# Ternary feed-forward block: the first layer of a group beside the second layer of the group before

## The reference, cut to what matters

```
W_fc: (1024, 256)   W_proj: (256, 1024)   ln_w, ln_b: (1024,)
absmean(W): gamma = mean(|W|) + 1e-6;  Ws = W / gamma
            sign(Ws) * min(round(|Ws|), 1)          # -1, 0 or 1
h = einsum('btd,hd->bth', layernorm(x), absmean(W_fc))
h = gelu(h, approximate=False)
h = (h - mean(h)) / sqrt(var(h) + 1e-5) * ln_w + ln_b
x = x + einsum('btd,dh->bth', h, absmean(W_proj))
```

## Time and profile before

| what | value |
|---|---|
| median of 3 runs | 3279.15 us (3278.52 to 3281.96) |
| profiled execution, its own time | 3280.81 us |
| span of its trace | 3278.7 us |
| mean granted TensorE clock | 0.904 of full speed |
| PE busy over the span | 2688.4 us (82%) |
| DVE, ACT, POOL busy | 1828.0, 1209.4, 793.0 us |
| block `l0f` in the trace | from 463.3 us to 680.4 us |

### The profile page before, as it was taken

How to read it: one execution, slowest core, us unless ns; L and a number is a source line. 1 busy time by engine, 2 the same in 40 slices (tenths; PEclk the granted TensorE clock), 3 DMA queues, 4 the chain that set the end, 5 groups by cost and what they waited for, 6 DMA issues and landing times. The chain is left out here.

```text
span 3278.7 us, 47320 instructions
## 1 busy us (share of the span) xinstructions
PE 2688.4 (82%) x15122; PEld 1841.3 (56%) x15123; DVE 1828.0 (56%) x3976; ACT 1209.4 (37%) x3052; POOL 793.0 (24%) x613
## 2 busy tenths in 40 slices
PE   3998977779777779599998979869867688879996
PEld 1565754457545446377776757546534466436664
DVE  6875963359787634344444559843343488433334
ACT  2323642236577513244343436511111366312211
POOL 4433520035200034122222236421100143131110
PEclk8999988899877779799999999879977798889998
DMA  9001000000200223200001020131110300321012
GB/s 290 1 1 44 12 17 0 0 14 1 56 4 4 36 86 111 84 1 1 1 1 46 11 65 1 66 133 31 39 51 0 78 14 1 139 105 32 31 32 96
DMA packets 158950, 142.27 MB, mean 43 GB/s; under 512 B 59012, under 2 KB 146068, under 8 KB 158388
## 3 DMA queue, kind: packets, MB, share of 16 engines
q1 hardware_dynamic: 145828, 111.95, 11.8%
q0 software_dynamic: 8688, 23.82, 2.0%
q10 hardware_dynamic: 4256, 4.20, 0.4%
HBM read 97.12 MB, written 42.81 MB: 43 GB/s over the span
## 5 line engine op out<-in xcount | busy, mean ns | idle before, releaser
L873 POOL TENSOR_TENSOR room<-room 128x1024 f32<-128x1024 f32 x144 | 273.3, 1898 | 454.2 <-DVE room L818 453.3
L812 DVE TENSOR_REDUCE room<-room 128x8 f32<-128x1024 f32 x144 | 174.0, 1208 | 0.0
L1312 PE MATMUL l3f_hidden<-room,Y 128*128 x312 | 146.1, 612 | 5.3 <-DVE Y L1552 4.9
L1331 PE MATMUL l3f_out<-room,Y 128*128 x624 | 141.1, 379 | 1.6 <-DVE Y L1577 1.6
L549 PE MATMUL l2a_proj<-room 128*128 128x256 f32 x512 | 128.7, 400 | 14.3 <-ACT room L896 14.3
L1331 PEld LDWEIGHTS l3f_out<-room,Y 128*128 128x128 f32 x624 | 118.5, 190 | 34.1 <-issue 20.0
L873 POOL TENSOR_TENSOR room<-room,l2a_rinv 128x1024 f32<-128x1024 f32 x32 | 60.7, 1897 | 253.4 <-DVE l2a_rinv L818 253.4
L549 PEld LDWEIGHTS l2a_proj<-room 128*128 128x128 f32 x512 | 97.3, 197 | 32.2 <-issue 17.0
L1688 POOL DMA_INDIRECT results<-Y,l3f_dest x39 | 37.5, 961 | 300.4 <-DVE Y L1585 165.3
L942 ACT ACTIVATE room<-l2a_scores,l2a_nmx 128x128 f32<-128x128 f32 x256 | 72.3, 381 | 93.6 <-DVE l2a_nmx L804 93.6
L2244 POOL DMA_INDIRECT sorted_rows<-room,l1f_place_i x32 | 31.6, 986 | 305.3 <-DVE l1f_place_i L1999 296.1
(11 more groups left out here) (740 smaller groups left out, 6829.6 us busy)
## 6 DMA issues: line engine op xcount, KB each, us to landing
sorted_rows<-zeros SPq DMA_DIRECT2D x1, 16512.0 KB, 67.5
room<-in_L_ffn_w SPq DMA_DIRECT2D x16, 1024.0 KB, 11.6
room<-in_L_ffn_W SPq DMA_DIRECT2D x16, 1024.0 KB, 12.0
Y<-sorted_rows SPq DMA_DIRECT2D x62, 129.0 KB, 2.1
room<-in_ctx SPq DMA_DIRECT2D x24, 256.0 KB, 2.7
room<-results SPq DMA_DIRECT2D x12, 512.0 KB, 7.4
room<-sorted_rows SPq DMA_DIRECT2D x39, 129.0 KB, 2.1
Y<-results SPq DMA_DIRECT2D x8, 512.0 KB, 5.9
```

Of the source, the lines that this page charges most:

```text
L812: dve.tensor_reduce(rsum[:, u % 2, :], p[:, u % (TURN + 1), :, :], AX.X, ALU.add)
L873: pool.tensor_tensor(p[:, u % (TURN + 1), :, :], p[:, u % (TURN + 1), :, :], rinv[:, u % (TURN + 1), :].unsqueeze(2).to_broadcast([P, HEAD ...
L1312: mm = pe.matmul(hbank[a][:, :], rowsT[:, par, kc, :], chip.room[:, bass.ds(at + (kc * F + a * half_f), half_f)], start=(kc == 0), stop=(k ...
L1331: mm = pe.matmul(obank[par][:, 0:D], hT[:, f, :], chip.room[:, bass.ds(at + (SLOT // 2 + f * D), D)], start=(f == 0), stop=(f == HC - 1))
```

## The change

The block is written out in `NG + 1 = 5` steps without loops. Step t does the first layer of group t and the second layer of group t - 1. `h` and `yT` get two copies, the transposes get four PSUM banks (`bank`), and the banks' use is counted by a table (`place`) made when the program is built. The two sums over partitions are two matmuls, `W_fc` is made ternary in two halves of 1024 columns, each with its own signal, the four bank fills of `W_fc` go in the order 0, 2, 1, 3, and `W_proj` is made ternary and transposed in the middle of step 0. The rows of the first group are normalised before the weights' thresholds, and those of group t + 2 in step t. `bn_aggr` is done with each added tile, and the root and reciprocal for the next block at the end of this one, so the block leaves "rstd". Activation tables are loaded by explicit `preload_act_table`.

```diff
-        WT = (FC * KC // 4)
-        PER = 1 + FC // 2
+        fills = [("y", 0, 0), ("y", 0, 1)] + [("fc", 0, q) for q in (0, 2, 1, 3)]
+        bank_of = {("fc", 0, q): b for q, b in ((0, 1), (2, 3), (1, 0), (3, 2))}
...
+            b = bank_of.get(x, x[2] % 4)
...
             @block.tensor
-                pe.wait_ge(mags_ready, 2)
-                pe.matmul(obank[0][:, 0:2], allones, rowsum[:, :], start=True, stop=True).then_inc(sums_ready, 1)
-                with pe.Fori(0, NG) as g:
...
+                turn_rows(0)
+                for m in range(2):
+                    pe.wait_ge(mags_ready, m + 1)
+                    pe.matmul(obank[m][:, 0:1], allones, rowsum[:, m:m + 1], start=True, stop=True).then_inc(sums_ready, 1)
+                    if m == 0:
+                        for q in (0, 2):
+                            turn_fc(q)
+                for q in (1, 3):
+                    turn_fc(q)
+                for t in range(NG + 1):
+                    a, c = t, t - 1
+                    for j in range(GR):
+                        if a < NG:
+                            first_layer(a, j)
+                        if j < 2 and c >= 0:
+                            for f in range(4 * j, 4 * j + 4):
+                                turn_hidden(c, f)
+                        if j == 1 and c < 0:
+                            for q in range(WT):
+                                turn_proj(q)
+                        if j == 2 and a + 1 < NG:
+                            turn_rows(a + 1)
+                    if c >= 0:
+                        for j in range(GR):
+                            second_layer(c, j)
...
             @block.vector
+                def add(b):
+                    dve.wait_ge(out_filled, b + 1)
+                    dve.tensor_tensor(chip.X[:, b, :], chip.X[:, b, :], obank[b % 2][:, 0:D], ALU.add).then_inc(out_added, 1)
+                    dve.drain()
+                    dve.bn_stats(chip.bn[:, b, :], chip.X[:, b, :])
+                    dve.drain()
+                    dve.bn_aggr(chip.mv[:, b, :], chip.bn[:, b, :])
+                normalise(0)
+                w.wait(dve)
+                empty_y(0)
+                threshold(0)
+                fc = w.v["fc"].rearrange("p c n -> p (c n)")
+                for i in range(2):
+                    ternary(0, fc, slice(i * HALF_W, (i + 1) * HALF_W)).then_inc(fc_ready, 1)
+                for q in (0, 2, 1, 3):
+                    if place[("fc", 0, q)][0] % 2 == 0:
+                        copy_fc(dve, q)
+                normalise(1)
+                threshold(1)
+                ternary(1, w.v["proj"].rearrange("p c n -> p (c n)"), slice(0, FC * D)).then_inc(proj_ready, 1)
+                for t in range(NG + 1):
+                    a, c = t, t - 1
+                    for j in range(GR):
+                        if a < NG and j:
+                            hidden_sums(a, j - 1)
+                        if j < 2 and c >= 0:
+                            for f in (4 * j, 4 * j + 2):
+                                empty_hidden(c, f)
+                        if j == 1 and c < 0:
+                            for q in (0, 2):
+                                copy_proj(dve, q)
+                        if j == 2 and a + 1 < NG:
+                            empty_y(a + 1)
+                            if a + 2 < NG:
+                                normalise(a + 2)
+                    if a < NG:
+                        hidden_sums(a, GR - 1)
+                        normalise_hidden(a)
+                    if c >= 0:
+                        for j in range(GR):
+                            add(c * GR + j)
+                dve.drain()
+                ln_stats_vector(chip, dve, chip.X, end, have="mv")
...
             @block.scalar
+                for m, src in enumerate((w.v["fc"], w.v["proj"])):
+                    act.activation(mag[:, :], src.rearrange("p c n -> p (c n)"), ACT.Abs, accum_out=rowsum[:, m:m + 1]).then_inc(mags_ready, 1)
+                    act.drain()
+                    if m == 0:
+                        empty_y(0)
+                for q in (0, 2, 1, 3):
+                    if place[("fc", 0, q)][0] % 2 == 1:
+                        copy_fc(act, q)
+                act.preload_act_table(ACT.Gelu)
+                for t in range(NG + 1):
+                    a, c = t, t - 1
+                    for j in range(GR):
+                        if a < NG:
+                            gelu(a, j)
+                        if j < 2 and c >= 0:
+                            for f in (4 * j + 1, 4 * j + 3):
+                                empty_hidden(c, f)
+                        if j == 1 and c < 0:
+                            for q in (1, 3):
+                                copy_proj(act, q)
+                        if j == 2 and a + 1 < NG:
+                            empty_y(a + 1)
+                    if a < NG:
+                        act.preload_act_table(ACT.Sqrt)
+                        act.wait_ge(hvar_ready, a + 1)
+                        act.activation(hstd[:, :], hvar[:, :], ACT.Sqrt).then_inc(hstd_ready, 1)
+                        if a + 1 < NG:
+                            act.preload_act_table(ACT.Gelu)
+                ln_stats_scalar(chip, act, end)
...
-LEAVES_STATS = {**{b: "rstd" for b in PLANS}, "rwkv": "rstd", "l1x": "rstd", "l1f": "rstd", "l2fm": "bn", **{b: "bn" for b in ("l0f", "gau")}}
+LEAVES_STATS = {**{b: "rstd" for b in PLANS}, "rwkv": "rstd", "l1x": "rstd", "l1f": "rstd", "l2fm": "bn", **{b: "bn" for b in ("gau",)}, "l0f": "rstd"}
```

More of the change, by code:

```diff
@@ L2545, in ternary_ffn_block @@
         hrstd = sb("hrstd", [P, GR])
-        tbank = [chip.ps(f"l0f_turn{i}", scope) for i in range(2)]
+        bank = [chip.ps(f"l0f_bank{i}", scope) for i in range(4)]
         hbank = [chip.ps(f"l0f_hidden{i}", scope) for i in range(2)]
@@ new lines, in first_layer @@
+                def first_layer(g, j):
+                    if j == 0:
+                        for kc in range(KC):
+                            wait_emptied(pe, ("y", g, kc))
+                    for c in range(2):
+                        n = (g * GR + j) * 2 + c
+                        if g == 0 and j == 0:
+                            for kc in range(KC):
+                                wait_emptied(pe, ("fc", 0, kc * 2 + c))
+                        if n >= 2:
+                            pe.wait_ge(gelu_done, n - 1)
+                        for kc in range(KC):
+                            mm = pe.matmul(hbank[c][:, :], yT[:, g % 2, kc, j * P:(j + 1) * P], fcT[:, kc, c * 512:(c + 1) * 512],
+                                           start=(kc == 0), stop=(kc == KC - 1))
+                        mm.then_inc(h_filled, 1)
@@ new lines, in turn_hidden, with second_layer @@
+                def turn_hidden(g, f):
+                    pe.wait_ge(hn_ready, g + 1)
+                    to, signal = wait_free(("h", g, f))
+                    for j in range(GR):
+                        mm = pe.transpose(to[:, j * P:(j + 1) * P], h[:, g % 2, j, f * P:(f + 1) * P], chip.ident[:, :])
+                    mm.then_inc(signal, 1)
+                def second_layer(g, j):
+                    n = g * GR + j
+                    if n == 0:
+                        for q in range(WT):
+                            wait_emptied(pe, ("proj", 0, q))
+                    if j == 0:
+                        for f in range(FC - 4, FC):
+                            wait_emptied(pe, ("h", g, f))
+                    if n >= 2:
+                        pe.wait_ge(out_added, n - 1)
+                    for f in range(FC):
+                        mm = pe.matmul(obank[j % 2][:, 0:D], hT[:, f, j * P:(j + 1) * P], projT[:, f, :], start=(f == 0), stop=(f == FC - 1))
+                    mm.then_inc(out_filled, 1)
```

231 lines of the change are left out of this document (111 added, 120 removed).

## The result

The changed kernel takes 3202.99 us (median of 4 runs, 3200.94 to 3203.83) against 3278.84 us (median of 4). The ratio is 0.9766 with a 95% interval of 0.9749 to 0.9783, so 71 to 82 us were saved. The forecast was 3210 us in a range of 3202 to 3230. The profiled execution took 3200.94 us, 79.9 less than the profiled one of before.

What follows compares the result with a forecast made beforehand. No engine was taken as the bound, but a chain through PE, ACT and DVE in turns. 3280.81 - 68.3 (block) - 0.75 (seam) = 3211.8 us, profiled execution 1.66 above the median, so 3210 us; range 3202 to 3230.

Steps and rivals of the forecast that it cites:

- The head: Block start up to the first hidden matmul: first weight half ready at 469.9, that matmul at about 474.
- T0: End of group 0's first layer, forecast at 492.0: 18.4 us of PE work from 469.9 plus 3.7 for lower clock.
- The stall: Step 1, before the hidden transposes: PE waits 2.6 us for DVE's normalisation, once, plus 1.5 us of lower clock.
- The steps: After group 0's first layer: steps 1 to 4 take 36.1, 32.0, 31.1 and 18.7 us, plus 1.2 for changes between kinds of work.
- The slack at the first addition: Second layer: DVE's first addition ends 0.4 us before PE wants its bank, after two output tiles.
- The seam: From the last row statistics to POOL's first attention instruction: 6.09 us before, a gain of 0.75.
- The clock rule: Skill's rule that idle gaps between matmul bursts lower the clock; taken strictly, it spares 1.5 us in step 1.
- The sum: Gain in the block, 68.3 us, plus 0.75 us at the passage to the next block.
- C: Rival: overlap isn't there, a wait in each step keeps rounds at 49 us; 3269 us, chance 0.05.
- B: Rival: PE stays at 1.2 GHz through the block's 131 us of work; slower than before, 3341 us, chance 0.02.
- A: Rival: DVE's chain 4 us late, PE waits in three steps' second layer; 16.5 us, 3227, chance 0.13.
- D: Rival: ACT reloads tables, up to six a step, mostly hidden; inside the forecast's range, chance 0.78 together with the forecast.

Runs made afterwards that it cites:

- W_fc in one piece: Changed kernel with W_fc made ternary in one pass instead of two halves; block 157.4 us against the changed kernel's 156.8.
- late additions: Changed kernel with three extra 1.29 us DVE passes between normalisation and additions in steps 1 to 3; block 171.3 us against 156.8.
- more cover: Changed kernel with two tiles' first layer ahead of step 1's hidden transposes, and copies awaited one by one; block 152.5 us against 156.8.
- two banks: Changed kernel with all transposes on two PSUM banks instead of four, overlap kept; block 169.6 us against 156.8.

## Why the prediction was right, point by point

**The head.** The first hidden matmul was forecast at about 474 and came at 473.39. The first weight transposes were forecast at 469.9 and came at 469.61.

**T0.** Forecast 492.0, measured 489.75. This is the term that was mis-sized: I allowed 3.7 us for the lower clock between 469.9 and T0, inside bounds of 2 to 6. From 469.61 to 489.75 are 20.1 us for 18.4 us of work, so it was 1.7, below the bounds. The stretch 473.40 to 490.00 shows a clock of 1.00, so nearly all of the first layer ran at the upper level. PE had worked almost without a break since 469.6 there, while the same stretch of the kernel before was a third idle.

**The stall.** 2.6 us forecast, 2.61 measured, once. The lower clock behind it: 1.5 forecast, and 7.04 us at 0.76 is a loss of 1.7. This hit is luck: the 1.5 was the middle of 0 and 2.9, and the same stall cost nothing in the run with W_fc in one piece.

**The steps.** 36.1, 32.0, 31.1 and 18.7 us forecast. The second layers' ends give 36.4 (489.75 to 526.19), 31.9 and 31.0, and the last step 5.2 us of transposes and 13.9 of second layer. The 1.2 us added for changes between kinds of work were not there: PE goes from one kind to the next with no gap, as in the full stretches above.

**The slack at the first addition.** 0.4 us by the sum, 0.4 in the trace, and the run with late additions shows what lies behind it. That DVE's 17.77 us of a round fit beside PE's 32.0 "many times over" was wrong: they fit once.

**The seam.** 0.75 us forecast, 0.84 measured.

**Tables of ACT.** GELU's table is loaded once a group and the root's once, and Identity and Copy run in between without a load, as the Trainium skill says ("ScalarE: Activation LUTs", section "Table sets: the hidden batching unit"):

```profile
492.65 1.28 ACT L2841 ACT_TABLE_LOAD   x1
...
497.09 0.78 ACT L2810 ACTIVATE room<-l0f_bank,vecs 128x512 f32<-128x512 f32 x1 [2.06 <-PE l0f_bank L2645]
...
509.14 0.59 ACT L2800 COPY room<-l0f_bank 128x512 f32<-128x512 f32 x1 [0.27 <-PE l0f_bank L2607]
...
510.86 0.60 ACT L2805 ACTIVATE room<-l0f_hidden 128x512 f32<-128x512 f32 x1 [1.13 <-PE l0f_hidden L2637]
```

The load at 492.65 is GELU's. Line 2810 is an Identity, line 2800 a Copy and line 2805 a GELU, and ACT's next load starts at 513.19.

**The clock rule.** Taken strictly, the rule of the Trainium skill ("TensorE: Matmul & The Clock Gate", section "HAM oscillation — how this bites in real kernels") would have spared the clock's loss behind a short stall. The row at 0.76 after 2.61 us does not agree; those at 1.00 after 1.25 and after 2.62 us do. So idles of one length were followed by either level, and the length of the last idle alone does not tell which.

**The sum.** Forecast for the block and its seam: 69.0 us; measured 71.9. Of the 2.9 us of difference 2.3 are T0 and 1.2 the changes between kinds, less what step 1 and the last transposes took more. The time came out 7 us below the forecast, and 2.9 of these are the block. The other 4 lie behind it, where two executions of one kernel differ by as much. The 3202.99 us lie only 1 us inside the range's lower end of 3202; the block's 2.9 us alone would have put them at about 3207. That the time is so near the edge, and still inside, is chance.

**The rivals.** C (the overlap isn't there) and B (PE stays at the lower level) are refuted by the stretches at 1.00 with PE busy throughout. A did not occur, by 0.4 us. D did not occur: ACT loads eight tables in the block, as before.

**What I had not asked.** The prediction took the round as a whole and never split its 17 us. The runs do: of 71.9 us the order of the groups gives 31.5, the early rows 19.5, the two further banks 8.8, and head, seam and loops 12.1 in this order of undoing. In the overlapped kernel the banks are worth 12.8 and the head 7.7, so the parts don't simply add. Both figures for the banks hold about 5 us of the head, where two fills in a row share a bank; with banks used by turns they might be smaller, and no run shows it.

## What to carry to other kernels

Where engines work in turns on one group, put one group's first half beside the previous group's second half, and then look for the engine that serves both: the reserve at its tightest wait (0.4 us here) tells how far it may fall behind, and each us beyond it is paid in every step. Work of the next group that depends on nothing, such as normalising and transposing its rows, is worth as much as its hole and the clock behind it, 6.5 us a round here for 0.9 us of matmuls. Where a stage is a small part of the kernel, compare the stage between two marks in the traces; here that agreed to 0.1 us between executions whose total times differed by 17. Then look once behind the second mark too: of 4.3 us gained in the block 1.6 were lost in the next one.

## What the runs showed of the hardware

The granted clock after a short idle of PE was 1.00 after 1.25 us. After 2.61 us it was 0.76 over the next 7 us in the changed kernel, and after 2.62 us it was 1.00 in the run with W_fc in one piece. In the block behind, one wait of 2.59 us left the clock at 1.00 in the changed kernel and brought 0.83 over 10 us with more cover. A wait of 3.38 us was followed by the full rate once and by a quarter more time once, one of 3.73 us by a quarter more. So a short stall has a price of nothing or of 1.6 to 1.8 us here (3.4 us with two banks), and its length did not tell which. Waits of under 1 us between the first transposes were enough to keep the first layer at the lower level for longer (9.33 against 7.03 us for two tiles). With seventeen transposes of a constant in the head the first weight transposes ran at the upper level, 1.09 instead of 1.97 us. And a stage whose code did not change, l1f, took 175.2 to 189.2 us, with one wait in it of 3.1 us in the shortest and of 15.0 in the longest.
